# Projection stage: mask rows stored before batch 0, block loads of two units issued by ScalarE, last weight sums and leading tiles reordered

## The chip, the cores and the metric

The kernel runs on one NeuronCore of a Trainium2 chip. The metric is the device time of one execution in microseconds (us), lower is better. The core has five engines with an instruction stream each: TensorE (PE in the profile) for matrix products, VectorE (DVE), ScalarE (ACT), GpSimd (POOL) and SyncE (SP), which here only waits and issues transfers. Sixteen DMA engines carry out the transfers. Engines run on their own and meet at semaphores.

## The reference, cut to what matters

A two-layer network over x of shape (8, 256, 512): cross attention, a quantized feed-forward, a gated long convolution and an FP8 feed-forward. The change touches the first part, the projection and the attention over it. There are 8 batches, 256 channels, 512 positions, 16 heads of 16 dimensions.

```
xn = layernorm(x)                      # over the last axis
q = Wq xn + bq;  k = Wk ctx + bk;  v = Wv ctx + bv
dot = q^T k / 4                        # per head
mask = target_mask x source_mask
dot = mask * dot - (1 - mask) * 1e6
out = (softmax(dot) * mask) v
x = x + tanh(g_xattn[0]) * out
# next layer: its weights are quantized with scale = mean(|w|) + 1e-5
```

The scale of the next layer's weights needs the sum of absolute values of three matrices. Those sums are taken in pieces during the projection.

## The kernel before, in words

**Projection** (phase_project) loops over the 8 batches. TensorE computes keys (line 376), queries (389) and values (401) in fp32. VectorE adds biases and masks (finish, line 444) and evacuates values (462). ScalarE and GpSimd split each q and k into three bf16 parts: part 1 (ScalarE, 318), rest 1 (GpSimd, 282), part 2 (ScalarE, 323), rest 2 (GpSimd, 288). SyncE stores the parts to HBM (store_parts, 200) and the masked values (store_values, 206). ScalarE also normalises the next batch's x (331), masks the values (341) and sums absolute weights, three pieces m = 0, 1, 2 per batch (sum_weights, 310); VectorE adds the pieces up (add_sums, 426). After the last batch TensorE sums over partitions with a matrix of ones (tensor_total, 420).

SyncE loads, in iteration b, the context of batch b + 3, and the mask and the weights of batch b + 2, each behind waits for buffers to come free.

**A unit** is half a batch: 8 heads. There are 16 units. Attention works on a stack of bf16 rows per unit, made of six blocks of parts (three leading, three rest) and mask rows. load_unit (63) reads it back from HBM: 4 mask rows (70), 12 block transfers of 128 KB (79) and, for the first two batches, 4 constant rows (85). The semaphore qk_lead tells that masks and leading blocks are there, qk_rest the others. The slot of a unit is one of four; those of units 2 and 3 lie over buffers of the projection. The mask rows themselves are first made by GpSimd (277, ready at about 9 us) and stored to HBM once (249), now behind batch 1; load_unit of unit 0 follows behind batch 1, that of unit 1 behind batch 3, that of unit 2 between the two last stores of parts (load_next, 580), that of unit 3 after them.

**Ahead work.** From batch 3 on, TensorE computes in pairs, between the products of the projection, the leading products of unit 0 and then unit 1 (tensor_pair, 791), and VectorE reduces each tile to row maxima (879). The maxima of a unit are split, turned by TensorE (777) and copied by ScalarE to a row (700 for unit 0, 706 later), which SyncE places into the stack (572). Ten tiles of unit 1 are left for after the projection (tensor_first, 780), in five pairs: a pair waits until both tiles of the pair before are reduced.

**Attention** has 8 steps per unit. In each, TensorE computes scores (824), ScalarE exponentials (731, two per step), TensorE the products with v (834), and TensorE and VectorE leading tiles of the next units. In steps 1 to 3 ScalarE also rounds a piece of the next layer's weights (745), which SyncE loads per unit (565); numerators are evacuated at step 4 and after the last one (720).

Each engine's order is written out by hand, and an engine works strictly in that order. ScalarE's order in batch b is: part 1 of K, normalise b + 1, sum 0, part 2 of K, part 1 of Q, sum 1, part 2 of Q, mask values, sum 2. In the last batch its three sums stand first and the copy of unit 0's maxima behind part 1 of K.

The functions that the diff touches, and what calls them:

Of the kernel before, what the change touches and what calls it, by code (L numbers as in the profile page):

```python
# [12 lines left out]
B = 8  # L13
# [49 lines left out]
def load_unit(core, sp, b, h):  # L63

    slot = 2 * (b % 2) + h
    sp.wait_ge(core.qk_stored[b % 2], 32 * (b // 2 + 1))
    for a in range(2):
        for dst, src in ((core.Q, core.mask_q), (core.K, core.mask_k)):
            heads = dst[slot][:, QUAD * a:QUAD * (a + 1), :]
            sp.dma_start(heads[SIDE * a + LEAD:SIDE * (a + 1):STEP],  # L70
                         src[:, b].unsqueeze(1).to_broadcast([HD, QUAD, L])).then_inc(core.qk_lead[slot], 16)
    planes = core.parts.rearrange("s b j c l -> (s b j) c l")
    for blk in range(BLOCKS):
# [8 lines left out]
    if b < 2:  # L82
        for a in range(2):
            for dst, src in ((core.Q, core.mask_q), (core.K, core.mask_k)):
                sp.dma_start(dst[slot][SIDE * (1 - a) + LEAD:SIDE * (2 - a):STEP, QUAD * a:QUAD * (a + 1), :],
                             src[BLOCKS:BLOCKS + 1, 0].unsqueeze(1).to_broadcast([HD, QUAD, L]))\
                    .then_inc(core.qk_rest[slot], 16)

# [45 lines left out]
def phase_project(core, ctx, A):  # L137
# [37 lines left out]
    def sync(sp, load_first, load_next):  # L175
# [56 lines left out]
        load_weights(1)  # L232
        for b in range(B):
# [12 lines left out]
            if b == 1:  # L246
                sp.wait_ge(rows_ready, 2)
                for side, dst in ((0, core.mask_q), (1, core.mask_k)):
                    sp.dma_start(dst.rearrange("r b (s n) -> (b s) r n", n=MN), rows8[:, side])\
                        .then_inc(rows_stored, 16)  # L250
                sp.wait_ge(rows_stored, 32)
                load_unit(core, sp, 0, 0)
            if b == 3:
                load_unit(core, sp, 0, 1)
# [42 lines left out]
    def scalar(act, rows_of_first_max):  # L297
# [50 lines left out]
        for b in range(B):  # L348
            if b == B - 1:
                for m in range(3):  # L350
                    sum_weights(b, m)
# [4 lines left out]
            if b == B - 1:  # L356
                rows_of_first_max(act)
# [5 lines left out]
            mask_values(b)  # L363
            if b < B - 1:
# [3 lines left out]
    def tensor(pe, ahead):  # L368
# [37 lines left out]
        for b in range(B):  # L406
# [8 lines left out]
            ahead(pe, b, 3)  # L415
    def tensor_total(pe):

        pe.wait_ge(f_ready, 2 * B)
# [9 lines left out]
    def vector(dve, ahead):  # L428
# [42 lines left out]
        for b in range(B):  # L471
# [9 lines left out]
            if b:  # L481
                values(b)
                add_sums(dve, b - 1)
            ahead(dve, b, 3)

    def vector_total(dve):

        add_sums(dve, B - 1)
        nc.vector.memset(ones[:], 1.0).then_inc(wrun_ready, 1)
# [1527 lines left out]
```

## Time and profile before

| what | us |
|---|---|
| median of 3 runs | 1270.89 |
| lowest, highest | 1264.79, 1272.02 |
| the profiled execution's own time | 1270.36 |
| its span in the profile | 1268.6 |
| projection, until its last ahead tiles | 0 to about 156 |
| first exponential (table load) | 174.69 |
| second unit of attention starts | about 201 |

Busy shares over the span are PE 85%, DVE 79%, ACT 55%, POOL 41%. They are averages over stages with different limits. How to read it: the profile lists one execution. A line of the time order has start, duration, engine, source line, operation, output <- inputs, shapes, count, and in brackets the idle time before it and what ended that. SPq rows are transfers being issued: their duration is SyncE's, not the transfer's. PEclk is the clock granted to TensorE, 1.00 for full speed and 0.50 for half; DMA is the mean busy share of the 16 engines.

### The profile page before, as it was taken

The numbers are of one execution on the slowest core, as the hardware profiler recorded it, in microseconds if no ns is written. First come the engines' busy times: TensorE is split into PE (matmuls) and PEld (weight loads), VectorE is DVE, ScalarE is ACT, GpSimd is POOL, SyncE is SP. The second block draws the span as 40 slices with busy tenths as digits, with TensorE's granted clock in tenths as the row PEclk, the third lists the DMA queues.
The fourth block names the chain that finished last, engine by engine and source line by source line (L and its number), as shares of the span: only waits on it lengthen the run. The fifth ranks groups of instructions, "written<-read, shape, count | busy, mean of one in ns | idle before, by whom it ended". The sixth has DMA issues, their size and how long they took to land. (4 is left out here: it accounts for less than half of the span.)

```text
span 1268.6 us, 14032 instructions
## 1 busy us (share of the span) xinstructions
PE 1077.1 (85%) x4802; PEld 422.0 (33%) x4802; DVE 995.9 (79%) x1521; ACT 695.6 (55%) x835; POOL 514.6 (41%) x403
## 2 busy tenths in 40 slices
PE   3849669999999999868999976999999997189586
PEld 2424312222222222124444433444444443034232
DVE  4337669999999999278999964888888888777898
ACT  2746648887888888946666552110000000686896
POOL 1645411534535535530011014878888883000021
PEclk8969869999999999999999996999999999599889
DMA  9779872545446444123111101111211110000011
GB/s 323 226 224 340 315 221 67 153 133 179 136 130 191 127 135 151 51 94 137 34 51 35 49 17 40 65 55 62 66 51 65 57 60 17 0 1 1 9 58 67
DMA packets 73703, 132.89 MB, mean 105 GB/s; under 512 B 18336, under 2 KB 37152, under 8 KB 73120
## 3 DMA queue, kind: packets, MB, share of 16 engines
q1 hardware_dynamic: 73632, 132.00, 32.5%
q8 instruction: 38, 0.62, 0.2%
q14 instruction: 33, 0.27, 0.1%
HBM read 107.58 MB, written 22.02 MB: 102 GB/s over the span
## 5 line engine op out<-in xcount | busy, mean ns | idle before, releaser
L879 DVE TENSOR_REDUCE mneg<-ps_m 128x1 f32<-128x512 f32 x512 | 326.8, 684 | 55.9 <-PE ps_m L791 52.2
L1452 PE MATMUL ps_y<-kv,toeplitz_sb 128*128 128x512 f32 x640 | 280.3, 597 | 9.5 <-POOL kv L1364 9.5
L731 ACT ACTIVATE probs<-ps_s 128x1024 f32<-128x1024 f32 x256 | 250.7, 1023 | 39.1 <-PE ps_s L824 39.1
L1452 PEld LDWEIGHTS ps_y<-kv,toeplitz_sb 128*128 128x128 f32 x640 | 121.4, 192 | 156.3 <-issue 156.3
L824 PE MATMUL ps_s<-qk_stack 128*128 128x512 bf16 x512 | 138.8, 386 | 23.1 <-ACT probs L731 22.0
L791 PE MATMUL ps_m<-qk_stack 64*128 64x512 bf16 x512 | 110.6, 395 | 37.5 <-DMA qk_stack<-qk_parts 21.8
L834 PE MATMUL ps_o<-probs,v_all 128*17 128x512 f32 x1024 | 135.5, 601 | 0.2 <-ACT probs L731 0.2
L1364 POOL TENSOR_TENSOR kv<-vT,ctxT_sb 128x2048 f32<-128x2048 f32 x32 | 118.7, 3709 | 40.1 <-PE ps_y L1452 33.3
L1070 PE MATMUL ps_g<-w,xT_f 128*128 128x512 bf16 x512 | 120.0, 383 | 11.4 <-DVE h_f L1236 7.9
L1417 ACT ACTIVATE w_anchor<-w_f 128x512 f32<-128x512 f32 x32 | 20.1, 628 | 180.6 <-DMA w_f<-in_w 180.6
L1518 DVE TENSOR_TENSOR z<-ps_y,ctxT_sb 128x1024 f32<-128x1024 f32 x64 | 77.9, 1218 | 48.1 <-PE ps_y L1452 48.1
L673 POOL TENSOR_TENSOR inv_all<-inv_all,mb_b 128x512 f32<-128x512 f32 x16 | 20.3, 1270 | 203.6 <-DMA inv_all<-inv_rows 203.6
L791 PEld LDWEIGHTS ps_m<-qk_stack 64*128 64x128 bf16 x512 | 27.1, 93 | 205.7 <-DVE mneg L879 144.3
L1267 POOL TENSOR_TENSOR X<-X,down_sums 128x512 f32<-128x512 f32 x16 | 20.5, 1282 | 173.5 <-ACT down_sums L1110 173.5
L1775 PE MATMUL ps_fp<-w 128*128 128x512 bf16 x256 | 66.5, 413 | 22.7 <-DVE w L1842 12.5
L1526 DVE TENSOR_REDUCE vT<-z 128x256 f32<-128x2304 f32 x32 | 81.7, 2553 | 1.1
L1122 ACT ACTIVATE sg_f<-ps_g,sc_f 128x512 f32<-128x512 f32 x64 | 43.8, 687 | 57.5 <-PE ps_g L1070 40.5
L1070 PEld LDWEIGHTS ps_g<-w,xT_f 128*128 128x128 bf16 x512 | 48.2, 98 | 69.3 <-DVE h_f L1236 12.4
L691 POOL TENSOR_SCALAR w<-w_sweep 128x512 bf16<-128x512 f32 x48 | 70.7, 1495 | 1.3
L96 DVE BATCH_NORM_STATS2 bn<-X 128x6 f32<-128x512 f32 x64 | 42.4, 682 | 36.5 <-DMA X<-in_x 15.0
L824 PEld LDWEIGHTS ps_s<-qk_stack 128*128 128x128 bf16 x512 | 35.8, 97 | 97.5 <-ACT probs L731 58.1
L1753 PE MATMUL ps_fp<-w 128*128 128x512 bf16 x256 | 59.0, 391 | 1.7 <-ACT w L1667 1.7
(163 smaller groups left out, 1613.9 us busy)
## 6 DMA issues: line engine op xcount, KB each, us to landing
qk_stack<-qk_parts SPq DMA_DIRECT2D x192, 128.0 KB, 2.9
w_sweep<-in_w SPq DMA_DIRECT2D x8, 1536.0 KB, 11.6
qk_parts<-qk_part SPq DMA_DIRECT2D x16, 768.0 KB, 6.1
w_sweep<-in_w SPq DMA_DIRECT2D x16, 768.0 KB, 5.6
w_sweep<-in_w SPq DMA_DIRECT2D x16, 512.0 KB, 3.6
toeplitz_sb<-in_toeplitz SPq DMA_DIRECT2D x32, 256.0 KB, 2.6
w_f<-in_w SPq DMA_DIRECT2D x32, 256.0 KB, 2.9
v_rows<-vp SPq DMA_DIRECT2D x8, 544.0 KB, 10.3
```

The costliest lines, as they stand in the source:

```text
L691: nc.gpsimd.tensor_scalar(core.w3[:, m].rearrange("p a b -> p (a b)")[:, u * L:(u + 1) * L], wc[:, h, m, :], MAGIC, None, ALU.subtract).th ...
L731: nc.scalar.activation(pr[:, k % 2, 2 * slot:2 * slot + 2, :], S[:, 2 * slot:2 * slot + 2, :], ACT.Exp).then_inc(exp_done, 1)
L791: nc.tensor.matmul(M[:, bank_, :], Q[slot][rows, hd, tc * P:(tc + 1) * P], K[slot][rows, hd, :], start=True, stop=True).then_inc(max_mm, 1)
L824: mm = nc.tensor.matmul(S[:, g, :], K[slot4][:, hd, (k % LT) * P:(k % LT + 1) * P], Q[slot4][:, hd, :], start=True, stop=True)
L834: mm = nc.tensor.matmul(O[32 * g:32 * g + HD + 1, :], V[:, par, sc, h * UH + 2 * g + G, :], pr[:, k % 2, g, :], start=(sc == 0), stop=(sc ...
L879: nc.vector.tensor_reduce(mneg[:, h, tc, hd:hd + 1], M[:, bank_, :], AX.X, ALU.max, negate=True).then_inc(max_red, 1)
L1070: mm = nc.tensor.matmul(G[:, c % 2, j, :], xT[:, par, k, :], wt[:, k, c * L:(c + 1) * L], start=(k == 0), stop=(k == LT - 1))
L1364: nc.gpsimd.tensor_tensor(kv[:, g % 2].rearrange("p l (b j i) -> p (l b) j i", b=B, j=GROUP), over_j(group(vT, g)), over_i(group(cT, g)), ...
L1452: mm = nc.tensor.matmul(Y[:, q % 3, l2, :], T[:, g % 2, (lt - m) * P:(lt - m + 1) * P], kv[:, g % 2, m, :], start=(m == 0), stop=(m == lt))
L1518: nc.vector.tensor_tensor(z[:, g % 2, NB // 2 * half:NB // 2 * (half + 1), :, 0:GROUP], Y[:, q % 3].rearrange("p l (b j i) -> p (l b) j i" ...
L1526: nc.vector.tensor_reduce(group(vT, g), z[:, g % 2], AX.X, ALU.add).then_inc(red_ready, 1)
L1775: mm = nc.tensor.matmul(D[:, r, :], h8[:, j % 4, L * t + r * P:L * t + (r + 1) * P], proj[:, ot, :], start=(i == 0 and t == 0), stop=(i == ...
```

## The change: what it does

1. The mask rows are stored ahead of batch 0, and SyncE waits for their landing behind batch 0.
2. load_unit is split into load_masks (with the constant rows) and load_blocks. For units 0 and 1 SyncE issues the masks behind batches 0 and 2; ScalarE issues the blocks, leading ones of unit 0 in batch 1, its rest in batch 2, those of unit 1 in batches 3 and 4, behind the masked values. For units 2 and 3, in load_unit, the constant rows now come ahead of the blocks.
3. In batch 7 ScalarE does one sum, the copy of the maxima, part 1 of K, then the two other sums. VectorE's last additions stand ahead of the last values, and the total follows the last ahead tiles directly, with a wait for the keys alone.
4. The ten leading tiles go one by one over three banks, each waiting for the tile two before it.
5. ScalarE's wait for the stored values moves from ahead of the first exponential to the first evacuation (step 4 of unit 0).

```
-def load_unit(core, sp, b, h):
+def load_masks(core, sp, b, h):
 
     slot = 2 * (b % 2) + h
-    sp.wait_ge(core.qk_stored[b % 2], 32 * (b // 2 + 1))
     for a in range(2):
         for dst, src in ((core.Q, core.mask_q), (core.K, core.mask_k)):
             heads = dst[slot][:, QUAD * a:QUAD * (a + 1), :]
             sp.dma_start(heads[SIDE * a + LEAD:SIDE * (a + 1):STEP],
                          src[:, b].unsqueeze(1).to_broadcast([HD, QUAD, L])).then_inc(core.qk_lead[slot], 16)
+            if b < 2:
+                sp.dma_start(heads[SIDE * (1 - a) + LEAD:SIDE * (2 - a):STEP],
+                             src[BLOCKS:BLOCKS + 1, 0].unsqueeze(1).to_broadcast([HD, QUAD, L]))\
+                    .then_inc(core.qk_rest[slot], 16)
+
+
+def load_blocks(core, sp, b, h, blocks):
+
+    slot = 2 * (b % 2) + h
+    sp.wait_ge(core.qk_stored[b % 2], 32 * (b // 2 + 1))
     planes = core.parts.rearrange("s b j c l -> (s b j) c l")
-    for blk in range(BLOCKS):
+    for blk in blocks:
...
-    if b < 2:
-        for a in range(2):
-            for dst, src in ((core.Q, core.mask_q), (core.K, core.mask_k)):
-                sp.dma_start(dst[slot][SIDE * (1 - a) + LEAD:SIDE * (2 - a):STEP, QUAD * a:QUAD * (a + 1), :],
-                             src[BLOCKS:BLOCKS + 1, 0].unsqueeze(1).to_broadcast([HD, QUAD, L]))\
-                    .then_inc(core.qk_rest[slot], 16)
+
+def load_unit(core, sp, b, h):
+
+    load_masks(core, sp, b, h)
+    load_blocks(core, sp, b, h, range(BLOCKS))
 
@@ -230,6 +235,9 @@ (SyncE)
         load_weights(1)
+        sp.wait_ge(rows_ready, 2)
+        for side, dst in ((0, core.mask_q), (1, core.mask_k)):
+            sp.dma_start(dst.rearrange("r b (s n) -> (b s) r n", n=MN), rows8[:, side]).then_inc(rows_stored, 16)
         for b in range(B):
...
             store_values(b)
-            if b == 1:
-                sp.wait_ge(rows_ready, 2)
-                for side, dst in ((0, core.mask_q), (1, core.mask_k)):
-                    sp.dma_start(dst.rearrange("r b (s n) -> (b s) r n", n=MN), rows8[:, side])\
-                        .then_inc(rows_stored, 16)
+            if b == 0:
                 sp.wait_ge(rows_stored, 32)
-                load_unit(core, sp, 0, 0)
-            if b == 3:
-                load_unit(core, sp, 0, 1)
+                load_masks(core, sp, 0, 0)
+            if b == 2:
+                load_masks(core, sp, 0, 1)
@@ -347,20 +351,23 @@ (ScalarE)
             if b == B - 1:
-                for m in range(3):
-                    sum_weights(b, m)
+                sum_weights(b, 0)
+                rows_of_first_max(act)
             part1(b, KS)
             if 1 <= b < B - 1:
                 normalise(b + 1)
                 sum_weights(b, 0)
             if b == B - 1:
-                rows_of_first_max(act)
+                sum_weights(b, 1)
+                sum_weights(b, 2)
             part2(b, KS)
...
             mask_values(b)
+            if 1 <= b < 5:
+                load_blocks(core, act, 0, (b - 1) // 2, range(LEAD) if b % 2 else range(LEAD, BLOCKS))
@@ -413,9 +420,11 @@ (TensorE)
             ahead(pe, b, 3)
+            if b == B - 1:
+                tensor_total(pe)
     def tensor_total(pe):
 
-        pe.wait_ge(f_ready, 2 * B)
+        pe.wait_ge(f_ready, nth(B - 1, KS))
@@ -479,14 +488,16 @@ (VectorE)
             if b:
+                add_sums(dve, b - 1)
+            if b == B - 1:
+                add_sums(dve, b)
+                nc.vector.memset(ones[:], 1.0).then_inc(wrun_ready, 1)
+            if b:
                 values(b)
-                add_sums(dve, b - 1)
             ahead(dve, b, 3)
 
     def vector_total(dve):
 
-        add_sums(dve, B - 1)
-        nc.vector.memset(ones[:], 1.0).then_inc(wrun_ready, 1)
@@ -707,11 +718,12 @@ (ScalarE in attention)
-        for p in range(2):
-            act.wait_ge(v_stored[p], 16 * (B // 2))
 
         def evacuate(u, h, G, bu):
             act.wait_ge(pv_step, STEPS * u + LT * (G + 1))
+            if u == 0 and G == 0:
+                for p in range(2):
+                    act.wait_ge(v_stored[p], 16 * (B // 2))
@@ -779,9 +791,9 @@
     def tensor_first(pe):
 
-        for q in range(AHEAD, 3 * TILES // 4):
-            tensor_pair(pe, q)
         pe.wait_ge(vt_ready, LT * B)
+        for tile in range(2 * AHEAD - TILES, HALF):
+            max_tile(pe, 1, 1, tile, HALF + tile)
         pe.wait_ge(o_cleared, 1)
@@ -796,7 +808,7 @@
-        elif TURN_SLOT <= j < TURN_SLOT + 2 or (v == 1 and j < 2):
+        elif TURN_SLOT <= j < TURN_SLOT + 2:
             pe.wait_ge(max_red, n - 1)
@@ -911,8 +923,8 @@
     def vector_first(dve):
 
-        for q in range(AHEAD, 3 * TILES // 4):
-            reduce_pair(dve, q)
+        for tile in range(2 * AHEAD - TILES, HALF):
+            reduce_tile(dve, 1, 1, tile, bank(HALF + tile))
```

## Rows read from the trace of the kernel before

**Rows 1.** Windows: stretch, length, busy PE PEld DVE ACT POOL, PEclk, DMA share, GB/s.
```profile
32.00:36.00 4.00, 4.00 (x8) 1.69 (x7) 0.69 (x2) 1.06 (x1) 2.83 (x2) 0.71 0.11 46
36.00:44.00 8.00, 8.00 (x25) 4.42 (x24) 3.87 (x7) 4.98 (x9) 4.79 (x3) 1.00 0.53 164
44.00:72.00 28.00, 15.27 (x48) 8.59 (x46) 8.31 (x18) 23.12 (x38) 17.12 (x8) 0.82 0.94 284
72.00:88.00 16.00, 6.96 (x14) 2.92 (x15) 1.96 (x4) 3.33 (x5) 4.24 (x2) 0.58 0.50 159
88.00:144.40 56.40, 48.29 (x153) 24.14 (x152) 41.02 (x72) 36.31 (x59) 29.69 (x14) 0.94 1.00 345
```

**Rows 2.** Time order of TensorE: start, us, engine, line, operation, [idle <- releaser].
```profile
81.04 0.61 PE L791 MATMUL ps_m<-qk_stack 64*128 64x512 bf16 x2 [21.77 <-DMA qk_stack<-qk_parts]
...
160.00 0.35 PE L420 MATMUL ps_a<-w_sums,w_ones 128*128 128x3 f32 x2 [4.11 <-DVE w_ones L489]
...
164.19 0.61 PE L791 MATMUL ps_m<-qk_stack 64*128 64x512 bf16 x2 [1.38 <-DVE mneg L879]
```

**Rows 3.** Time order of ScalarE, batches 2, 4 and 7 and the first exponentials.
```profile
58.37 1.04 ACT L318 ACTIVATE qk_part<-qk_f 128x1024 bf16<-128x1024 f32 x1
...
98.66 1.06 ACT L318 ACTIVATE qk_part<-qk_f 128x1024 bf16<-128x1024 f32 x1 [2.11 <-DVE qk_f L444]
...
107.43 1.06 ACT L323 ACTIVATE qk_part<-qk_f 128x1024 bf16<-128x1024 f32 x1 [2.34 <-POOL qk_f L282]
...
109.99 1.04 ACT L310 ACTIVATE w_junk<-w_sweep 128x1024 bf16<-128x1024 f32 x1
...
144.38 1.06 ACT L310 ACTIVATE w_junk<-w_sweep 128x1024 bf16<-128x1024 f32 x1 [0.85 <-DMA w_sweep<-in_w]
...
147.80 1.04 ACT L318 ACTIVATE qk_part<-qk_f 128x1024 bf16<-128x1024 f32 x1
148.75 0.57 ACT L700 ACTIVATE mrow<-ps_m 16x512 bf16<-16x512 bf16 x1
...
174.69 1.28 ACT L731 ACT_TABLE_LOAD   x1 [15.60 <-DMA v_rows<-vp]
...
179.97 0.80 ACT L745 ACTIVATE w_sweep<-w_sweep,columns 128x512 f32<-128x512 f32 x1
```

**Rows 4.** Time order of SyncE's queue: start and duration of issues.
```profile
36.56 0.37 SPq L200 DMA_DIRECT2D qk_parts<-qk_part  x1
...
46.54 0.47 SPq L206 DMA_DIRECT2D v_rows<-vp  x1
...
52.68 0.37 SPq L200 DMA_DIRECT2D qk_parts<-qk_part  x1
...
61.35 8.10 SPq L249 DMA_DIRECT2D mask_k<-mask_row  x1
...
75.27 7.58 SPq L79 DMA_DIRECT2D qk_stack<-qk_parts  x12
...
154.36 0.38 SPq L200 DMA_DIRECT2D qk_parts<-qk_part  x1
...
169.63 1.04 SPq L565 DMA_DIRECT2D w_sweep<-in_w  x1
```

**Rows 5.** Landings by line: L249 both, L206 issued at 60.2, L565 at 169.6.
```profile
DMA to landing us min/median/max: 10.6/10.9/11.3
...
DMA to landing us min/median/max: 9.5/9.5/9.5
...
DMA to landing us min/median/max: 7.0/7.0/7.0
```

**Rows 6.** Line 317, ScalarE's sequencer: the wait ahead of batch 5's part 1.
```profile
L317 ACTq EVENT_SEMAPHORE  x1: 17/17/17, 107.9 to 107.9; - x1
```

**Rows 7.** Waits from 60 to 150 us: total, times, longest.
```profile
ACT qk_part L318 <- DVE qk_f L444: 23.0, 4, 13.4
```

**Rows 8.** Line 79 from 60 to 140 us: issue ns min/median/max.
```profile
L79 SPq DMA_DIRECT2D qk_stack<-qk_parts x24: 532/592/596, 75.3 to 115.1; - x24
```

More of the change, by code:

```diff
@@ L497, in phase_project @@
     last = (p3_ready, k_done, v_done, q_done, f_ready, vt_ready, wsum_ready, w_step, qk_stored, v_stored)
-    return Phase(sync, gpsimd, scalar, tensor, vector), tensor_total, vector_total, last
+    return Phase(sync, gpsimd, scalar, tensor, vector), vector_total, last
 def phase_attention(core, ctx, A, before):
@@ L1926, in build @@
             pass
-        pj, tensor_total, vector_total, last = phase_project(core, ctx, A)
+        pj, vector_total, last = phase_project(core, ctx, A)
         at, first, *tail = phase_attention(core, ctx, A, last)
@@ L1954, in _ @@
                 pj.tensor(pe, tensor_ahead)
-                tensor_total(pe)
                 tensor_first(pe)
```

## The prediction

> **What bounds it now.** I read the stage table (windows) first, then the time order of TensorE, ScalarE and SyncE's queue around each long wait, then single lines' durations and landings. The edits touch only the projection and the start of attention; the chain that ended last lies a thousand us later, so the question is how much earlier attention reaches its steady pace.
>
> The windows show two halves of one stage [rows 1]. From 72 to 88 us TensorE is busy 7 of 16 us at a granted clock of 0.58, and the 16 DMA engines are busy half the time. From 88 to 144.4 us they are busy 1.00 of the time: there the projection is bound by transfers, not by TensorE.
>
> Three waits stand out. TensorE sits 21.8 us, until 81.04, for the first blocks of unit 0 [rows 2]. ScalarE's first sum of batch 7 waits for its weights until 144.38 [rows 3]: they come last of the loads, so the transfers' total decides when batch 7 can be finished. And the first exponential waits 15.6 us for the last values to be stored, until 174.69 [rows 3].
>
> **The change, part by part.**
>
> *Mask rows ahead of batch 0.* The second of their two stores, at 61.35, held SyncE 8.10 us [rows 4] and landed 11.3 us after its issue, at 72.7 [rows 5]. The values stored just before, issued at 60.2, landed 9.5 later, at 69.7 [rows 5]. So the rows cost about 3.0 us of transfers, and the first block could be issued only at 75.27 [rows 4]. Now they are the first thing behind the opening loads, near 20 us; from 32 to 36 us the engines are busy 0.11 [rows 1], those loads are through, and the rows fit there. If SyncE is held 8.10 us again, it is from 20 to 29, and its next work comes at 36.56 [rows 4]: cost nothing; without that cover, 8.10 us.
>
> *Masks and blocks of units 0 and 1.* SyncE issues eight mask transfers after batches 0 and 2, ScalarE six block transfers after each of batches 1 to 4. Twelve blocks take SyncE 7.58 us, 0.63 each [rows 4], so eight masks are 5.1 us of SyncE. After batch 0 they follow the values' store at 46.54 + 0.47 and end at 52.2, before the next store at 52.68 [rows 4]: hidden. ScalarE issues the six lead transfers of unit 0 by about 61 us. Before, the sixth went out at 75.27 + 5 x 0.63 = 78.4 and TensorE started at 81.04, 2.6 later, at half-busy engines; at full ones I allow 4. TensorE comes to them at 59.3 (81.04 less 21.77) [rows 2], so it waits about 5 us, not 21.8.
>
> *What it costs ScalarE.* No DMA is issued by ScalarE in this trace. The dearest reading takes SyncE's 0.63 in full: 6 x 0.63 = 3.8 us more per batch. The cheapest is that it is hidden. A row between them decides: the wait at line 317, which stands in the program behind the second part of Q, four mask products and a weight sum, is passed by ScalarE's sequencer at 107.9, while the engine has just started that second part at 107.43 [rows 3, 6]. So issuing starts at about 107.8 and ends at 111.6, while the engine has work until 109.99: 1.6 us more per batch. A sum takes 1.14 (three of them 3.42, 144.38 to 147.80), so an undisturbed batch lasts from 98.66 to 109.99 + 1.14 = 111.13, 12.47 us [rows 3]. Batch 2 began at 58.37, so batch 7 could begin at 58.37 + 5 x 12.47 + 4 x 1.6 = 127.1 (136.0 at 3.8 each). ScalarE's waits before, 23.0 us for the finished keys and queries in this stretch [rows 7], are the cover.
>
> *When the last weights land.* From 36 to 144.4 us the transfers idle 3.8 + 1.7 + 8.0 + 0 = 13.5 us [rows 1]. The 3.8 between 36 and 44 stays, since nothing has been computed yet that could be stored. The 8.0 of the stall is refilled, and the mask rows' 3.0 have left the stretch: 11.0. I take off 1.0 for idle that comes anew, since stores wait for a ScalarE that is 1.6 us per batch longer. Batch 7's first sum then starts at 144.38 - 10.0 = 134.4, above ScalarE's own 127.1. The bounds: 8.4 (ScalarE at 3.8 per group, 136.0) and 16.5 (all idle and the mask rows). So the stall of 21.8 is worth 10, because transfers take its place.
> A sentence apart: the Trainium skill, in "DMA: Bandwidth & Descriptors", section "Issuing engines are not separate DMA queues", says that DMAs issued by SyncE and ScalarE run on the same 16 engines and that a second issuer saves only issue time. By that rule the 88 to 144.4 stretch gains nothing from the new issuer; without it, one could hope for the whole 21.8, 1243.6 with the tail below.
>
> *Batch 7 in another order.* Before, three sums stood ahead of part 1 of K, which began at 147.80, 3.42 after the first sum; now one sum and the copy of the maxima, 1.14 + 0.57 = 1.7 [rows 3]. That is 1.7 us earlier. From part 1 to the store of K's parts is 154.36 - 147.80 = 6.56 as before [rows 3, 4]. Store: 134.4 + 1.7 + 6.56 = 142.7, 11.7 earlier. VectorE's last additions, now ahead of the values, wait for the third sum, about 138.3, while the values' products end near 142 (below): nothing.
>
> *Leading tiles and the total.* TensorE was done at 160.00 - 4.11 = 155.89, 6.6 behind the copy of the maxima, then sat 4.11 us before the total; its ten tiles went in pairs of 0.61 + 1.38 = 1.99 us [rows 2]. One at a time over three banks TensorE's and VectorE's work overlaps: between 5 x 0.61 = 3 (TensorE alone) and the 9.9 as it was; I take 7, VectorE having most of the 1.99. The total itself, now ahead of them, is two small products. With the copy done at 136.1 the products of values end at 142.7; the tiles, behind VectorE's values, clearing and scales (some 2.5 us), end near 152, and the scores follow.
>
> *The wait for stored values moved.* The first exponential no longer waits for it, so behind its table load it starts near 154 rather than at 174.69 + 1.28 = 175.97. But ScalarE's next wait is late next: after the exponentials of step 1 it rounds weights (line 745) that SyncE loads at 169.63, behind the whole of unit 2's loads, 15.27 us after the store of K's parts, landing 7.0 later [rows 4, 5]. That order is unchanged. New landing: 142.7 + 22.3 = 165.0. The two steps of exponentials are done by about 159, so ScalarE waits there 6 us. Before, the line ran at 179.97, 3.3 after the landing [rows 3]. Gain at that line: 15.0. The stored values themselves land two us before those weights and are asked for only at step 4: hidden. The row of maxima for unit 1 can be placed by SyncE behind two units' loads, at 142.7 + 31 = 174, nine us after ScalarE's wait, and is wanted with unit 1, six steps after it: hidden.
> TensorE idles before 165 and may come back at the lower clock, as it was in the stall [rows 1]; against that it is one step of products ahead. I take zero, bounds -1.4 and +1.4 (one idle of TensorE behind a pair, either way).
>
> **Sum.** 10.0 + 1.7 + 3.3 = 15.0 us. The profiled execution took 1270.36, 0.53 under the median shown. 1270.4 - 15.0 = 1255.4.
>
> **The rivals.**
> *ScalarE is held for all of its issuing.* 3.8 per group instead of 1.6: 10.0 becomes 8.4, 1257.0. For it, 0.63 on SyncE; against it, the sequencer that runs ahead [rows 6]. Chance 0.15.
> *Transfers gain less.* The refilled idle comes back elsewhere, because what SyncE may issue next is bound to computed parts, and fourteen of these transfers move into 44 to 72 us, where the engines are at 0.94 already [rows 1]. Then 4 instead of 10 stay: 1261.4. Chance 0.16.
> *The weights aren't late.* If they landed with the first steps, the exponential's whole advance would count, 175.97 - 154 = 22.0, and 1.4 for the step ahead: 1247.0. The rows of SyncE's order speak against it. Chance 0.08.
> *Slower: ScalarE stands still on a full queue.* SyncE was held 8.10 us by the mask rows' store [rows 4]. ScalarE issues into the same stretch of full engines. Held h us per group, batch 7 begins at 127.1 + 4h; at h = 5.6 the whole gain is gone, at 8.8 it is 1% slower; at 8.1 it gives 1280. Against it: the blocks issued by SyncE from 108 to 116, at full engines, took at most 0.60 each [rows 8]. Chance 0.09.
> A sentence apart: the Trainium skill, in "Perfetto Trace Analysis", section "Per-instruction lifecycle", says that such issues hold a shared descriptor generator under a lock, so that SyncE and ScalarE could delay each other; by it groups that met SyncE's eight masks would cost up to double, 3.8 us more each, which stays below 5.6.
>
> **Numbers.** Forecast 0.45, the rest 0.07 unnamed. One per cent is what can be told from no change here: the border is 1258.2. Faster: most of 0.45, half of the first rival, the third, 0.60; slower 0.09; same 0.31. The range takes in all but the slow rival and stray cases: 1246 to 1267; the forecast's own is 1251 to 1260.
>
> **What would show it.** TensorE's wait at about 59 us falls to under 8 us; the engines are near 1.00 from 50 to 134; ScalarE's group issues take 3.8 us with gaps of 1 to 2 us ahead of the third weight sum; the last weight load lands at 133 to 135; the store of K's parts stands at 143; the first exponential near 154, then a wait of about 6 us at the rounding of weights, released by the weights' load. I'm wrong if that wait is absent, if ScalarE shows gaps of over 5 us behind its issues, or if unit 1 starts later than 20 us behind the second wait.

## The result, and the profile after

The changed kernel takes 1253.36 us (median of 4 runs, 1249.34 to 1253.38); the one before, in the same series, 1271.09 (1264.79 to 1272.02). The ratio is 0.9863, 95% interval 0.9826 to 0.9900. The profiled execution took 1253.38 us at a span of 1251.6, 17.0 under the one before.

The windows of the kernel after, with the columns of [rows 1] (line numbers from here on are those of the changed kernel, if nothing else is said):

```profile
32.00:36.00 4.00, 4.00 (x11) 1.85 (x10) 2.44 (x3) 2.06 (x2) 2.83 (x2) 1.00 0.61 78
36.00:44.00 8.00, 8.00 (x28) 5.00 (x27) 3.23 (x5) 5.57 (x11) 4.52 (x3) 1.00 0.70 222
44.00:72.00 28.00, 22.33 (x60) 11.21 (x58) 12.22 (x24) 19.59 (x32) 17.12 (x8) 0.88 1.04 355
72.00:88.00 16.00, 14.98 (x53) 7.78 (x52) 11.52 (x22) 10.37 (x17) 8.47 (x4) 1.00 1.01 349
88.00:144.40 56.40, 43.45 (x130) 21.42 (x128) 36.49 (x69) 40.61 (x65) 34.12 (x16) 0.90 0.90 311
```

The hole from 72 to 88 us is gone: TensorE is busy 15.0 of 16 us at the full granted clock (2.4 GHz) where it was busy 7.0 at 0.58, and the DMA share went from 0.50 to 1.01. The stretch ahead of it moved 355 GB/s, not 284. The last one now has a share of 0.90: 0.95 until 128 us, where it had been 1.00, and less behind that, since the projection is through before its end.

TensorE in time order; answers to [rows 2]:

```profile
63.19 0.61 PE L803 MATMUL ps_m<-qk_stack 64*128 64x512 bf16 x2 [5.67 <-DMA qk_stack<-qk_parts]
...
140.28 0.35 PE L429 MATMUL ps_a<-w_sums,w_ones 128*128 128x3 f32 x2 [1.29 <-DVE w_ones L494]
141.46 0.39 PE L803 MATMUL ps_m<-qk_stack 64*128 64x512 bf16 x1 [0.83 <-DVE vt L471]
```

The stall fell from 21.77 to 5.67 us, and the wait ahead of the total from 4.11 to 1.29.

ScalarE in time order; answers to [rows 3]. L314 sums a weight, L322 is part 1, L711 copies the first maxima, L743 is the exponential, L757 rounds ternary weights. ACTq are the DMAs that ScalarE issues:

```profile
58.04 1.06 ACT L314 ACTIVATE w_junk<-w_sweep 128x1024 bf16<-128x1024 f32 x1 [2.23 <-issue]
59.09 1.04 ACT L322 ACTIVATE qk_part<-qk_f 128x1024 bf16<-128x1024 f32 x1
...
73.61 1.06 ACT L314 ACTIVATE w_junk<-w_sweep 128x1024 bf16<-128x1024 f32 x1 [2.92 <-issue]
...
87.77 1.06 ACT L314 ACTIVATE w_junk<-w_sweep 128x1024 bf16<-128x1024 f32 x1 [1.68 <-issue]
...
97.94 2.22 ACTq L88 DMA_DIRECT2D qk_stack<-qk_parts  x2
100.19 3.54 ACTq L88 DMA_DIRECT2D qk_stack<-qk_parts  x4
103.77 1.06 ACT L314 ACTIVATE w_junk<-w_sweep 128x1024 bf16<-128x1024 f32 x1 [3.36 <-issue]
...
130.89 0.57 ACT L711 ACTIVATE mrow<-ps_m 16x512 bf16<-16x512 bf16 x1
131.36 1.04 ACT L322 ACTIVATE qk_part<-qk_f 128x1024 bf16<-128x1024 f32 x1
...
149.56 1.28 ACT L743 ACT_TABLE_LOAD   x1 [6.42 <-PE ps_s L836]
...
162.98 0.81 ACT L757 ACTIVATE w_sweep<-w_sweep,columns 128x512 f32<-128x512 f32 x1 [7.80 <-DMA w_sweep<-in_w]
```

Four gaps of 1.7 to 3.4 us, one behind each group of six issues, 10.2 us in all, are what ScalarE pays. The first exponential comes 25 us earlier, and the engine then stands 7.80 us at the rounding of weights, which now ends last there.

SyncE's queue; answers to [rows 4]:

```profile
20.50 13.63 SPq L240 DMA_DIRECT2D mask_k<-mask_row  x1
36.15 0.36 SPq L205 DMA_DIRECT2D qk_parts<-qk_part  x1
...
137.92 0.38 SPq L205 DMA_DIRECT2D qk_parts<-qk_part  x1
...
153.29 0.95 SPq L576 DMA_DIRECT2D w_sweep<-in_w  x1
```

The rows' second store held SyncE 13.63 us, and its next work came 2 us later still. The store of K's parts stands at 137.92, 16.4 earlier than before; the ternary weights are issued 15.37 behind it. Their landing answers to [rows 5]:

```profile
DMA to landing us min/median/max: 9.7/9.7/9.7
```

### The profile page after: what moved, and what is told of

Its sections match the earlier page's. It is cut to its first block and busy times, and to the rows that moved or that the text cites. A ratio compares the mean times of both kernels' runs of the same rounds, so it can differ in the third digit from the quotient of the medians.

```text
span 1251.6 us, 14018 instructions
## 1 busy us (share of the span) xinstructions
PE 1082.8 (87%) x4802; PEld 423.3 (34%) x4802; DVE 995.8 (80%) x1521; ACT 695.9 (56%) x835; POOL 514.6 (41%) x403
## 5 line engine op out<-in xcount | busy, mean ns | idle before, releaser
L743 ACT ACTIVATE probs<-ps_s 128x1024 f32<-128x1024 f32 x256 | 250.9, 1022 | 38.3 <-PE ps_s L836 38.1
L803 PE MATMUL ps_m<-qk_stack 64*128 64x512 bf16 x512 | 113.6, 397 | 18.7 <-issue 6.2
L1082 PEld LDWEIGHTS ps_g<-w,xT_f 128*128 128x128 bf16 x512 | 48.1, 98 | 68.7 <-DVE h_f L1248 12.4
L101 DVE BATCH_NORM_STATS2 bn<-X 128x6 f32<-128x512 f32 x64 | 42.5, 683 | 35.7 <-DMA X<-in_x 14.6
```

Of the source, the lines that this page charges most:

```text
L743: nc.scalar.activation(pr[:, k % 2, 2 * slot:2 * slot + 2, :], S[:, 2 * slot:2 * slot + 2, :], ACT.Exp).then_inc(exp_done, 1)
L803: nc.tensor.matmul(M[:, bank_, :], Q[slot][rows, hd, tc * P:(tc + 1) * P], K[slot][rows, hd, :], start=True, stop=True).then_inc(max_mm, 1)
L1082: mm = nc.tensor.matmul(G[:, c % 2, j, :], xT[:, par, k, :], wt[:, k, c * L:(c + 1) * L], start=(k == 0), stop=(k == LT - 1))
```

## The experiments

Twelve kernels, three rounds each. The kernel before took 1271.73 us (median) beside the first four, 1271.12 beside the next four and 1271.61 beside the last four. A ratio is to the kernel before; every kernel has its own line numbers. The table has, in us, the start of batch 7's first sum, of the store of K's parts, of the first rounding of ternary weights (ScalarE) and of unit 1's first exponential, each from the one profiled execution, and the median time of all runs. The second unit of the kernel before starts at 199.2, a little ahead of the "about 201" given above.

| kernel | first sum | K's store | rounding | unit 1 | time |
|---|---|---|---|---|---|
| before | 144.38 | 154.36 | 179.97 | 199.2 | 1271.1 |
| changed | 129.83 | 137.92 | 162.98 | 180.9 | 1253.4 |
| rows alone | 133.65 | 143.63 | 169.34 | 188.4 | 1256.6 |
| rows late | 140.83 | 148.93 | 172.26 | 190.3 | 1261.0 |
| units on SyncE | 131.86 | 139.95 | 163.51 | 182.7 | 1255.2 |
| groups on SyncE | 129.07 | 137.18 | 161.33 | 180.4 | 1250.6 |
| groups in a gap | 126.32 | 134.43 | 158.77 | 177.8 | 1250.5 |
| sums back | 131.33 | 141.30 | 165.57 | 183.6 | 1254.9 |
| wait back | 130.08 | 138.18 | 163.87 | 182.8 | 1254.6 |
| weights first | 128.76 | 136.87 | 150.55 | 173.2 | 1245.8 |
| gap and weights | 126.23 | 134.33 | 151.47 | 170.7 | 1241.5 |
| maxima between | 124.95 | 133.05 | 150.18 | 169.3 | 1241.8 |
| pairs back | 129.43 | 137.53 | 161.41 | 180.5 | 1250.5 |
| constants behind | 130.54 | 138.63 | 163.38 | 182.8 | 1253.0 |

**One part alone: the mask rows.** The kernel before, with only the two row stores ahead of batch 0:

```diff
 (before)
+        sp.wait_ge(rows_ready, 2)
+        for side, dst in ((0, core.mask_q), (1, core.mask_k)):
+            sp.dma_start(dst..., rows8[:, side]).then_inc(rows_stored, 16)
         for b in range(B):
...
             if b == 1:
-                sp.wait_ge(rows_ready, 2)
-                for side, dst in ...: sp.dma_start(...)
                 sp.wait_ge(rows_stored, 32)
                 load_unit(core, sp, 0, 0)
```

> The kernel before with the first edit alone: the two stores of mask rows stand ahead of batch 0, SyncE still issues all masks and blocks behind the values' stores of batches 1 and 3. Theory A (the rows' own store and its landing were half of the 21.8 us stall, and the transfers fill what TensorE loses): the stall falls to 10 to 13 us, batch 7 begins 4 to 6 us earlier, 1266 us. Rival 1 (the whole shorter stall counts): 1261 us. Rival 2 (it was the last weights' landing alone that counted, unchanged): 1271 us.

Measured: 1256.55 us, ratio 0.9885 (0.9868 to 0.9901). TensorE, ScalarE (its first sum of batch 7) and SyncE of this kernel, then one window:

```profile
73.86 0.61 PE L790 MATMUL ps_m<-qk_stack 64*128 64x512 bf16 x2 [14.73 <-DMA qk_stack<-qk_parts]
```

```profile
133.65 1.06 ACT L309 ACTIVATE w_junk<-w_sweep 128x1024 bf16<-128x1024 f32 x1 [1.35 <-DMA w_sweep<-in_w]
```

```profile
143.63 0.38 SPq L200 DMA_DIRECT2D qk_parts<-qk_part  x1
```

```profile
72.00:88.00 16.00, 13.63 (x39) 6.74 (x40) 8.15 (x14) 7.87 (x13) 8.36 (x4) 0.81 1.04 342
```

Theory A and its rivals all expected too little. The stall still lasts 14.7 us, only 7.0 shorter, and yet batch 7 begins 10.7 us earlier (144.38 to 133.65). The window shows why: the transfers run at 1.04 through 72 to 88, where they had 0.50, so 8.6 us of idle transfers are refilled while TensorE partly stands; the rows' own transfers have left the stretch as well. By this trace what counted was the idle of the transfers, not that of TensorE. By the medians this one edit gives 14.6 us (1271.12 less 1256.55) of 17.7. The execution in the trace took 1259.29, the slowest of its four runs; it is 11.1 under the profiled one of the kernel before, of 17.0, and that is what batch 7 (10.7) and unit 1 (10.8) show. So alone the edit gives two thirds of the gain or more.

**The same part taken away.** The changed kernel with the rows back behind the values' store of batch 1, and unit 0's masks behind them:

```diff
-        sp.wait_ge(rows_ready, 2)
-        for side, dst in ...: sp.dma_start(...)       (ahead of batch 0)
...
-            if b == 0:
+            if b == 1:
+                sp.wait_ge(rows_ready, 2)
+                for side, dst in ...: sp.dma_start(...)
                 sp.wait_ge(rows_stored, 32)
                 load_masks(core, sp, 0, 0)
```

> The changed kernel with the mask rows back at their old place: their two stores stand behind the values' store of batch 1 and unit 0's masks behind them; ScalarE still issues the blocks early and the rest of the change stays. Theory A (the rows are most of the gain: TensorE needs the masks too, which land near 81, and stands still about 21 us from 59.3 as before): batch 7 begins near 142 and the time is 1264 to 1267 us. Rival (blocks already loaded during the stall keep the transfers full, so the later half of the projection catches up): batch 7 begins near 135 and the time is 1257 to 1259 us.

Measured: 1260.96 us, ratio 0.9916 (0.9901 to 0.9931), 7.6 slower than the changed kernel. It fell between the two theories. TensorE and one window of this kernel:

```profile
82.43 0.61 PE L804 MATMUL ps_m<-qk_stack 64*128 64x512 bf16 x2 [23.64 <-DMA qk_stack<-mask_k]
```

```profile
72.00:88.00 16.00, 5.57 (x8) 2.29 (x9) 1.29 (x2) 5.49 (x8) 4.27 (x3) 0.50 0.68 185
```

The releaser is now a mask, not a block. Theory A was right on the stall and on batch 7 (its first sum at 140.83, against 144.38 before), but 3 to 6 us too slow on the time: batch 7's own order and the missing wait for stored values still gave their part behind it. With the rows late the blocks' move refills 2.9 us of transfers (0.68 against 0.50) and moves batch 7 by 3.6.

**The other part taken away.** The changed kernel, with whole units loaded by SyncE behind batches 1 and 3 again:

```diff
-            if 1 <= b < 5:
-                load_blocks(core, act, 0, (b - 1) // 2, ...)
...
-            if b == 0:
+            if b == 1:
                 sp.wait_ge(rows_stored, 32)
-                load_masks(core, sp, 0, 0)
-            if b == 2:
-                load_masks(core, sp, 0, 1)
+                load_unit(core, sp, 0, 0)
+            if b == 3:
+                load_unit(core, sp, 0, 1)
```

> The changed kernel without its move of masks and blocks: the mask rows are stored ahead of batch 0 and everything else of the change stays, but SyncE issues the whole loads of units 0 and 1 behind the values' stores of batches 1 and 3, as before. With the mask rows alone the store of K's parts came at 143.63 and the time was 1256.55; the other order of batch 7 is worth 1.9 us of it. Theory A (what ScalarE's and the earlier masks' issues buy is the rest, between 141.8 and 137.9): the store near 141.8, 1257 us. Rival (the move buys nothing that reaches the end, since the transfers are full either way): 1253.4 to 1254.5 us.

Measured: 1255.20 us, ratio 0.9868 (0.9854 to 0.9883); the changed kernel's interval, 0.9826 to 0.9900, covers it. The stall is 16.4 us long again:

```profile
73.79 0.61 PE L801 MATMUL ps_m<-qk_stack 64*128 64x512 bf16 x2 [16.42 <-DMA qk_stack<-qk_parts]
```

```profile
44.00:133.00 89.00, 69.80 (x212) 34.20 (x210) 53.73 (x94) 62.19 (x101) 51.05 (x24) 0.90 0.99 332
```

The transfers are as full as in the changed kernel (its share from 44 to 133 is 0.99 too). Batch 7's first sum stands at 131.86, 2.0 later than the 129.83 of the change, and the time differs by 1.8 us, which these runs can't tell from nothing. The rival is nearer. So the part that looks largest, twenty-four transfers moved to another engine, removes 11 us of TensorE's stall and is worth 0 to 2 us.

Two things are mixed in that small number. The shorter stall is one; ScalarE's 10.2 us of gaps, which this kernel doesn't have and the changed one has, are the other. The two kernels that follow take the gaps away.

**Who issues the blocks.** SyncE issues the groups of batches 1 to 4, behind the values' store of each:

```diff
 (ScalarE)
-            if 1 <= b < 5:
-                load_blocks(core, act, 0, (b - 1) // 2, ...)
 (SyncE, behind store_values(b) and the masks)
+            if 1 <= b < 5:
+                load_blocks(core, sp, 0, (b - 1) // 2, ...)
```

> The changed kernel, but the four groups of block loads are issued by SyncE behind the stored values of the same batches instead of by ScalarE. Theory A (from batch 2 on the projection is bound by ScalarE, whose four groups left gaps of 2.2, 2.9, 1.7 and 3.4 us, 10.2 in all): the gaps go, batch 7's first sum is then held by its weights' landing, 127 to 128 instead of 129.8 (2 to 3 us), total 1250 to 1252. Rival B (the second issuer is what gained): SyncE's later stores and mask loads stall VectorE, 1256 to 1260. Theory C (transfers alone bound it): 1253, no change.

Measured: 1250.64 us, ratio 0.9840 (0.9820 to 0.9859). ScalarE's waits from 44 to 135 us have no more row for "issue", but this one:

```profile
ACT qk_part L324 <- DVE qk_f L453: 8.4, 3, 6.4
```

10.2 us of gaps went and 8.4 of waits for VectorE's keys and queries came; batch 7 begins at 129.07, 0.8 earlier, where theory A had 127 to 128. The time is the one of theory A, but the intervals of the two kernels overlap. TensorE's stall is 13.85 us here, and the kernel is no slower for it:

```profile
72.68 0.61 PE L803 MATMUL ps_m<-qk_stack 64*128 64x512 bf16 x2 [13.85 <-DMA qk_stack<-qk_parts]
```

The Trainium skill, in "DMA: Bandwidth & Descriptors", section "Issuing engines are not separate DMA queues", says that DMAs of every issuer run on the same 16 engines and that a second issuer saves only the time to initiate. Both kernels agree: with one issuer the time is no longer.

**The same issues in a gap of ScalarE.** ScalarE waits 2.34 to 2.52 us for GpSimd ahead of part 2 of Q in each batch; its group is issued there:

```diff
                 sum_weights(b, 1)
+            if 1 <= b < 5:
+                load_blocks(core, act, 0, (b - 1) // 2, ...)
             part2(b, QS)
             mask_values(b)
-            if 1 <= b < 5:
-                load_blocks(...)
```

> The changed kernel, but ScalarE issues each group of six ahead of part 2 of Q, where it waits 2.3 to 2.5 us for GpSimd, instead of behind the masked values. Theory A (ScalarE-bound, and its sequencer runs ahead of the engine): the issuing lies beside sum 1 and that wait, the gaps of 10.2 us in all shrink to under 3; blocks land 4 to 5 us earlier, so TensorE's wait of 5.7 us shrinks too; batch 7's first sum moves from 129.8 to the weights' landing, 125 to 128: 2 to 5 us faster, 1249 to 1251. Rival B (transfers bound it): no change, 1253. Rival C (the issues hold part 2 of Q back): 1256.

Measured: 1250.46 us, ratio 0.9838 (0.9818 to 0.9859), as theory A had it. One group there, TensorE's wait for the first blocks, and the sum's wait that is left (waits, 44 to 135 us):

```profile
60.11 1.19 ACTq L88 DMA_DIRECT2D qk_stack<-qk_parts  x2
```

```profile
58.97 0.39 PE L803 MATMUL ps_m<-qk_stack 64*128 64x512 bf16 x2 [1.48 <-DMA qk_stack<-qk_parts]
```

```profile
ACT w_junk L314 <- DMA w_sweep<-in_w: 1.4, 2, 0.8
```

The gaps are gone and batch 7 begins at 126.32, 3.5 earlier than in the changed kernel. Now ScalarE waits for weights again, 1.4 us, and 5.0 for VectorE's keys and queries: the bounds lie side by side. The time is 2.9 us below the changed kernel's median, but the runs of the two overlap (1249.35 to 1253.01 and 1249.34 to 1253.38); the trace shows the step, and the kernel with both edits, further down, confirms it.

Beside the kernel with whole units on SyncE this one shows what the shorter stall is worth without the gaps: TensorE's wait for blocks falls from 16.42 to 1.48 us, batch 7 begins 5.5 us earlier (131.86 to 126.32), the DMA share from 44 to 133 us is 1.02 in place of 0.99, and the time is 4.7 us lower. A third of the stall reached batch 7; in the changed kernel the gaps ate most of that.

**Batch 7's order.** The changed kernel with all three sums ahead of K's part 1 and the copy of the maxima behind it:

```diff
-                sum_weights(b, 0)
-                rows_of_first_max(act)
+                for m in range(3):
+                    sum_weights(b, m)
             part1(b, KS)
...
-                sum_weights(b, 1)
-                sum_weights(b, 2)
+                rows_of_first_max(act)
```

> The changed kernel, but in batch 7 all three weight sums stand ahead of the first part of K again, and the copy of the maxima behind it. Theory A (batch 7 of ScalarE is on the path to the store of K's parts): the first part of K begins near 133.2 instead of 131.4, since two sums of 1.14 come in and a copy of 0.57 goes out, the store comes 1.8 later and the time is 1255.2 us. Rival (the sums cost nothing there, something else sets the store): 1253.4 us and the store at 137.9.

Measured: 1254.90 us, ratio 0.9878 (0.9861 to 0.9896).

```profile
141.30 0.38 SPq L205 DMA_DIRECT2D qk_parts<-qk_part  x1
```

The store is 3.4 later, 1.5 of it from a batch 7 that began later in this trace (131.33); 1.9 are the order. The time moved by 1.5, on theory A's side but inside the intervals. The traces show the step, the times alone don't.

**The wait for stored values, put back** ahead of the first exponential:

```diff
         act.wait_ge(v_done, B)
+        for p in range(2):
+            act.wait_ge(v_stored[p], 16 * (B // 2))
...
-            if u == 0 and G == 0:
-                for p in range(2):
-                    act.wait_ge(v_stored[p], 16 * (B // 2))
```

> The changed kernel, but ScalarE's wait for the stored values stands ahead of the first exponential again. Theory A (what holds the start of attention is the landing of unit 0's weights at 162.95, behind which ScalarE sat 7.8 us): the first exponential starts behind the values' landing at 158.2 and its table load, near 159.5, two steps end at 163.6, so rounding starts 0.7 us later than now: 1254.1 us, within 1 us of the changed kernel. Rival B (the moved wait is worth its whole advance, 149.6 to 158.2): 8.7 us slower, 1262.

Measured: 1254.60 us, ratio 0.9869 (0.9848 to 0.9889).

```profile
158.59 1.28 ACT L742 ACT_TABLE_LOAD   x1 [15.19 <-DMA v_rows<-vp]
...
163.87 0.80 ACT L756 ACTIVATE w_sweep<-w_sweep,columns 128x512 f32<-128x512 f32 x1
```

A wait of 15.19 us is back, and the rounding of weights, without a wait now, comes 0.9 us later. Taking the largest wait of ScalarE away bought about 1 us in the traces, because the weights' landing stood right behind it; the 1.2 us between the medians are less than the runs can tell.

**The weights first.** SyncE loads the first ternary weights ahead of unit 2's masks and blocks:

```diff
         if h == 0:
+            sp.wait_ge(k_done, B)
+            sp.wait_ge(v_done, B)
+            load_weights(sp, 0, 0)
             sp.wait_ge(wsum_ready, 3 * B)
             load_unit(core, sp, 1, 0)
         else:
-            sp.wait_ge(k_done, B)
-            sp.wait_ge(v_done, B)
-            load_weights(sp, 0, 0)
```

> The changed kernel, but SyncE issues the weights of attention's unit 0 ahead of unit 2's masks and blocks (behind the same waits for the projection's last products) instead of behind them. Theory A: they land near 144 to 146 instead of 162.95, ScalarE's wait of 7.8 us at the rounding goes, the next thing it can meet are the stored values (near 159.5, wanted near 164), so 6 to 8 us faster: 1246. Rival B: the wait only changes its name (values, the row of maxima of unit 1 or the slots' loads are late in its place): 0 to 2 us, 1252.

Measured: 1245.75 us, ratio 0.9800 (0.9782 to 0.9819): 7.6 us under the changed kernel. ScalarE, then TensorE:

```profile
150.55 0.81 ACT L757 ACTIVATE w_sweep<-w_sweep,columns 128x512 f32<-128x512 f32 x1
```

```profile
172.15 1.89 PE L836 MATMUL ps_s<-qk_stack 128*128 128x512 bf16 x4 [3.67 <-DMA qk_stack<-mrow]
```

The wait at the rounding is gone, which comes 12.4 us earlier; part is given back where TensorE waits 3.67 us for unit 1's maxima, placed by SyncE behind all of unit 3.

**Both together.** The weights first and the issues in the gap:

> The changed kernel with two edits together: ScalarE issues its groups of blocks ahead of the second part of Q, and SyncE loads the first ternary weights of attention ahead of unit 2's masks and blocks. Alone they took 2.9 and 7.6 us off. Theory A (both act on one path one after the other, the first brings the store of K's parts forward, the second shortens what follows it): they add, 1242.9 us, the store of K's parts near 134.5, no wait of ScalarE at the rounding of the weights. Rival (behind the weights SyncE's queue is the next bound, and most of the first edit is lost there): 1245.5 us, as with the second alone.

Measured: 1241.46 us, ratio 0.9772 (0.9756 to 0.9788); the interval lies wholly below that of the change. The runs of this kernel (1240.71 to 1244.33) also lie below all of the weights first alone (1244.97 to 1247.37): the place of the issues is worth 4.3 us there. The store of K's parts and the weights behind it:

```profile
134.33 0.39 SPq L205 DMA_DIRECT2D qk_parts<-qk_part  x1
134.83 0.47 SPq L576 DMA_DIRECT2D w_sweep<-in_w  x1
```

They add, as theory A had it: 2.9 and 7.6 from 1253.36 make 1242.9. The 3.67 us wait is 0.25 in this trace.

**The maxima between the blocks.** As the last one, with unit 1's maxima placed behind eight of unit 3's sixteen blocks:

```diff
-            load_unit(core, sp, 1, 1)
+            load_masks(core, sp, 1, 1)
+            load_blocks(core, sp, 1, 1, range(BLOCKS // 2))
+            place_max(sp, 1, 1, 1)
+            load_blocks(core, sp, 1, 1, range(BLOCKS // 2, BLOCKS))
             load_weights(sp, 1, 1)
...
 (unit 1's maxima are left out where SyncE placed them before)
```

> The two edits together, and SyncE places the maxima of unit 1 between the eighth and the ninth block of unit 3, no longer behind all sixteen and a weight load. In the kernel with the weights first, TensorE waited 3.67 us for that placement near 168.5. Theory A (SyncE's order is what is late there): the wait goes, and 3.7 us with it, 1239.2 us against the two edits alone at 1242.9. Rival (the maxima land early and TensorE waits for the next thing, the weights of unit 1 or the values): as the two edits alone, 1242.9.

Measured: 1241.84 us, ratio 0.9769 (0.9754 to 0.9783), the same. Theory A missed: with both edits that wait had already shrunk, and there was nothing to take.

**Leading tiles in pairs again.** The changed kernel with the ten tiles in pairs over two banks, ahead of the wait for the last values:

```diff
-        pe.wait_ge(vt_ready, LT * B)
-        for tile in range(2 * AHEAD - TILES, HALF):
-            max_tile(pe, 1, 1, tile, HALF + tile)
+        for q in range(AHEAD, 3 * TILES // 4):
+            tensor_pair(pe, q)
+        pe.wait_ge(vt_ready, LT * B)
...
 (VectorE's reductions in pairs too; one wait of the steps' tiles as before the change)
```

> The changed kernel with the ten leading tiles behind the projection in pairs over two banks again, ahead of the wait for the last values. Theory A (what ends last there is the weights' landing near 163, with 7.8 us to spare at the exponentials): the first exponential comes 2 to 3 us later and ScalarE's wait at the rounding of the weights shrinks by as much, 1253.4 us. Rival (the tiles' time reaches the end by way of TensorE's step ahead): 1256 us.

Measured: 1250.54 us, ratio 0.9834 (0.9812 to 0.9856).

```profile
148.69 1.28 ACT L743 ACT_TABLE_LOAD   x1 [6.43 <-PE ps_s L836]
...
161.41 0.81 ACT L757 ACTIVATE w_sweep<-w_sweep,columns 128x512 f32<-128x512 f32 x1 [7.66 <-DMA w_sweep<-in_w]
```

Not slower, as theory A said, though the first exponential isn't later (148.69 against 149.56), where 2 to 3 us were expected. VectorE's last values, first here, then in the changed kernel, and TensorE ahead of them in the changed kernel:

```profile
135.75 1.42 DVE L471 TENSOR_TENSOR vt<-ps_a,bv_rows 128x256 f32<-128x256 f32 x4 [0.16 <-PE ps_a L408]
```

```profile
140.06 1.35 DVE L471 TENSOR_TENSOR vt<-ps_a,bv_rows 128x256 f32<-128x256 f32 x4
```

```profile
131.55 0.61 PE L803 MATMUL ps_m<-qk_stack 64*128 64x512 bf16 x2 [6.21 <-issue]
132.09 3.78 PE L408 MATMUL ps_a<-w_qkv,cx 128*128 128x256 f32 x8
```

From the end of the last values to the first exponential are 11.5 us with the pairs and 8.2 without: the tiles do cost 3.4 more, as expected. But the last values end 4.2 us earlier here. In the changed kernel's trace TensorE idled 6.21 us before them and came back slow: eight products of values took 3.78 us, 1.99 here, where the idle was 0.59. What that idle waited for the trace doesn't show. Whether the pairs are better by 1 to 3 us stays open.

**Constant mask rows behind the blocks.** Units 2 and 3 of the changed kernel:

```diff
 (load_masks)
-            if b < 2:
+            if b < 1:
                 sp.dma_start(heads..., src[BLOCKS:BLOCKS + 1, 0]...)
 (load_unit, at its end)
+    if b == 1:
+        (the four constant rows)
```

> The changed kernel with the constant mask rows of units 2 and 3 issued behind each unit's blocks, as before the change, and no longer in between its masks. The landing of the first ternary weights took 9.66 us in the changed kernel and 7.0 in the one before. Theory A (the order among a unit's transfers doesn't reach that landing, since sixteen blocks of 128 KB lie in front of it either way): landing 9 to 10 us, 1253.4 us. Rival (the constant rows, which go out right behind the weights in the changed kernel, hold it up): landing 7 us, 1250.7 us.

Measured: 1252.98 us, ratio 0.9848 (0.9834 to 0.9863); the weights' landing:

```profile
DMA to landing us min/median/max: 9.5/9.5/9.5
```

As theory A had it. What makes this load take 7.1 us in one kernel and 9.7 in another was not found.

## Why the prediction was right

The forecast was 15.0 us, the profiled executions differ by 17.0, and the mechanism at the end is the one that was named: ScalarE waits for the ternary weights. Two terms were off, in opposite directions, one by 4.6 us too little and one by 2.8 too much; that the sum is off by only 2.0 is in part luck. By the prediction's steps:

*Mask rows.* Cost nothing: right, with SyncE held 13.63 us, not 8.10 [rows 4]; cover was enough by 2 us. Their worth was undersold: counted as 3.0 us of transfers inside another step, they are the largest part of the change (14.6 us alone by the medians, 11.1 by the profiled executions, 7.6 when taken back).

*Masks and blocks.* The wait at 59 us was to fall to about 5; it is 5.67.

*What it costs ScalarE.* 1.6 us a batch was forecast, within 0 and 3.8. The gaps are 10.2 us in four batches, 2.55 each: issuing began as early as thought, 0.18 us behind the start of part 2 in batch 4, but six issues took 4.0 to 5.8 us and not 3.8. A batch without a gap lasts 12.44 (part 1 of K at 104.83 and, a batch later, at 117.27), 12.47 forecast. ScalarE's own bound for batch 7, 127.1, became 129.83.

*When the last weights land.* This is the step that failed in size. They were to start batch 7 at 134.4; it starts at 129.83, a gain of 14.55 where 10.0 stood, and the weights had landed at 127.97, so ScalarE was last, not the transfers. Landing came 16.4 us earlier than [rows 3] has it; the upper bound given was 16.5. The idle of 36 to 44 us was held for fixed, but the share rose from 0.53 to 0.70 (1.4 us); and a share of 0.94 from 44 to 72 was taken for nearly full, but it rose to 1.04 (2.8 us). With the stall's window (0.50 to 1.01, 8.2 us) and the rows' 3.0 that makes 15.4. Against it stands idle that came anew, forecast as 1.0: the share from 88 to 128 us is 0.95, where it was 1.00 (2.0 us). The 13.4 that are left fall 3.0 short of the 16.4, since a busy share isn't a rate: from 44 to 72 us the share rose by a tenth and the rate by a quarter (284 to 355 GB/s). By the rates it closes: the 288 GB/s from 36 to 144.38 us before, moved at the 334 from 36 to 128 us after, take 93.5 us and not 108.4, 14.9 less, and 0.5 MB fewer are moved.

*Batch 7's order.* 1.7 forecast, 1.9 measured. From part 1 to the store 6.56 us, as [rows 3, 4].

*Leading tiles.* 7 us forecast, from 141.46 to 148.4 in the trace; that it buys nothing was in the price of the step after it.

*The wait moved.* First exponential near 154: it is 150.84 (149.56 plus the table). Then a wait of 6 us for the ternary weights: it is 7.80, and ends at 162.98, not 165.0. The store was 4.8 earlier than forecast, but the load took 9.66 us and not 7.0 [rows 5], which ate 2.7 of it. Gain at that line 16.99 against 15.0. So the sum was 10.0 + 1.7 + 3.3, and should have been 14.55 + 1.9 + 0.5. Unit 1 starts 18.3 us earlier, and 1.3 us of that are lost over the rest of the kernel; where was not looked for.

*The rivals.* Full holding of ScalarE: its issues do take 4.0 to 5.8 us a group, but the gaps are half of that. Transfers gaining less: refuted, batch 7 begins 14.55 us earlier and not 4. A full queue: no group held ScalarE for more than 3.36 us of idle, where 5.6 per group was the point at which the gain would be gone. Weights that aren't late, 1247.0: not in this kernel, but SyncE's order made it true in the one with the weights first, at 1245.75. The rule of the Trainium skill on a shared descriptor generator ("Perfetto Trace Analysis", section "Per-instruction lifecycle") was not tried: ScalarE's groups, from 53.2, 68.5, 83.6 and 97.9 us on, met none of SyncE's masks, issued from 45.44 to 51.10 and from 75.79 to 81.43.

## What to carry to other kernels

When transfers bound a stage, count a stall by the transfers that idle in it, not by the engine that stands: 15 us less of TensorE's stall were worth 5.5 at batch 7 here, where the transfers were nearly as full before, and 11 less were worth 0 to 2 when the engine that issued the blocks paid for them in gaps. Look at what a long wait hides before paying for its removal, since the next item of an in-order queue may stand right behind it; reordering that queue (three lines here) gave 7.6 us, where the removal of a 15 us wait had given about 1. And put an engine's DMA issues where it waits anyway.

## What the runs showed of the hardware

The second rows' store (128 KB) held SyncE for 8.10 us in the kernel before, 9.07 with the rows late, and 13.46 to 13.89 when issued near 20 us. The DMA share while it did so was 1.05, 0.98 and, in the changed kernel, 0.97: how full the transfers were doesn't explain the difference, and what does was not found.

Six block issues took ScalarE 4.0 to 5.8 us in the changed kernel, single ones up to 1.65, and 3.6 us in the gap ahead of part 2 of Q (the first two 1.19), at much the same DMA share (0.99 and 1.02 from 44 to 133). The longest one, at 98.51 us, met no issue of SyncE, which issued nothing between 96.71 and 101.05. Why the place matters was not tested.

The load of the first ternary weights, 1.5 MB, took 7.0 us from issue to landing before, 9.7 after, and 7.1 with the wait for stored values back, with the DMA engines full in both of the last two (share 1.00 and 1.01 from 153.3 to 160.5 us). The other kernels that left it behind unit 2's loads had 7.2 to 9.5, without a pattern that was found.
